# Layer 0's second pass: transposes with both partial sums side by side in place of a folding product

## The reference, cut to what matters

```python
for l in range(n_layers):
    x = jnp.concatenate([h[src], e], axis=1)
    x = x @ W1[l].T + b1[l]
    mu = jnp.mean(x, axis=0)
    var = jnp.var(x, axis=0)
    x = (x - mu) * jax.lax.rsqrt(var + BN_EPS) * gamma[l] + beta[l]
    x = jax.nn.relu(x)
    m = x @ W2[l].T + b2[l]
    h = jax.ops.segment_sum(m, dst, num_segments=n_nodes)
```

## Time and profile before

| | |
|---|---|
| median of 3 runs | 3245.53 us (3243.82 to 3248.12) |
| the profiled execution, its own time | 3253.43 us |
| its span, first to last instruction | 3252.2 us |
| busy share of the span: TensorE, VectorE, ScalarE, GpSimd | 82%, 60%, 41%, 66% |
| mean granted TensorE clock | 0.90 |
| the second pass of layer 0 | 1690.9 to 1869.2 us of the span |

### The profile page before, as it was taken

The page is one execution under the profiler, slowest core; times in us unless marked ns, Lnnn a source line. Parts: engine busy times, 40 slices in busy tenths (PEclk is TensorE's granted clock), DMA queues, the critical chain, the costliest instruction groups (busy, mean ns, idle before and its releaser), DMA issues.

```text
span 3252.2 us, 62180 instructions
## 1 busy us (share of the span) xinstructions
PE 2658.7 (82%) x14706; PEld 1830.4 (56%) x14706; DVE 1961.7 (60%) x3607; ACT 1331.8 (41%) x3295; POOL 2156.6 (66%) x2211
## 2 busy tenths in 40 slices
PE   6689896676777878888889998787879778877998
PEld 2234444555655567677766665555557556655444
DVE  7999585544444567777779965555546555555111
ACT  4877544433333446666657732222223222223111
POOL 4777776777777677777757747777755777774000
PEclk6799997877667889899989999999989999998999
DMA  4333646655555489999958845555535555554100
GB/s 144 103 107 107 199 130 187 189 168 160 166 164 149 136 288 326 319 326 325 324 160 312 295 150 159 155 157 157 158 113 173 156 156 158 156 157 155 52 1 20
DMA packets 305078, 570.49 MB, mean 175 GB/s; under 512 B 54465, under 2 KB 140406, under 8 KB 303510
## 3 DMA queue, kind: packets, MB, share of 16 engines
q1 hardware_dynamic: 204582, 299.39, 29.4%
q0 software_dynamic: 86528, 219.09, 23.1%
q10 hardware_dynamic: 13824, 50.34, 3.9%
HBM read 465.21 MB, written 103.66 MB: 175 GB/s over the span
## 4 chain that ended last, share of the span: by engine, by line
POOL 40%; PE 28%; issue 16%; DVE 7%; DMA 4%; DVEq 2%; ACT 2%; SPq 0%; POOLq 0%; ACTq 0%
POOL region L534 20%; POOL tN L534 11%; PE psum L959 9%; POOL tA L534 9%; PE psum L611 4%; DVE region L1491 2%; PE psum L1216 2%; PE psum L625 2%; PE psum L1205 2%; PE psum L917 1%; PE psum L772 1%; DVEq L1484 1%; PE psum L932 1%; DMA tN<-tabs,region 1%; PE psum L783 1%
## 5 line engine op out<-in xcount | busy, mean ns | idle before, releaser
L534 POOL DMA_INDIRECT region<-tab,region x624 | 601.3, 964 | 271.3 <-issue 197.3
L1205 PE MATMUL psum<-w_all,region 128*128 128x256 f32 x2496 | 632.4, 399 | 3.1 <-DVE small L1894 2.4
L1205 PEld LDWEIGHTS psum<-w_all,region 128*128 128x128 f32 x2496 | 482.1, 200 | 67.1 <-issue 3.8
L2607 POOL DMA_INDIRECT by_tile<-stage,place x416 | 408.5, 982 | 167.6 <-issue 129.1
L657 ACT COPY win_turned<-psum 128x128 f32<-128x128 f32 x210 | 55.7, 265 | 803.4 <-PE psum L641 803.4
L534 POOL DMA_INDIRECT tN<-tab,region x312 | 299.7, 961 | 95.0 <-issue 94.7
L534 POOL DMA_INDIRECT tA<-tab,region x312 | 296.5, 950 | 95.0 <-issue 94.7
L611 PE MATMUL psum<-region 128*64 128x256 f32 (+1 forms) x1664 | 222.5, 392 | 165.6 <-DVE region L2010 97.4
L1216 PE MATMUL psum<-region 128*128 128x256 f32 x1040 | 281.1, 417 | 78.3 <-DVE region L1871 72.4
L1216 PEld LDWEIGHTS psum<-region 128*128 128x128 f32 x1040 | 206.9, 206 | 132.4 <-issue 101.4
L2005 DVE TENSOR_TENSOR psum<-region,psum 128x1024 f32<-128x1024 f32 x104 | 127.9, 1229 | 212.2 <-DMA region<-tab,region 201.4
(11 more groups left out here) (423 smaller groups left out, 5251.4 us busy)
## 6 DMA issues: line engine op xcount, KB each, us to landing
region<-e_t SPq DMA_DIRECT2D x416, 256.0 KB
region<-by_tile SPq DMA_DIRECT2D x131, 264.0 KB
stage<-e_rows SPq DMA_DIRECT2D x208, 132.0 KB
pre_dram<-region ACTq DMA_DIRECT2D x48, 512.0 KB, 6.0
pre_dram<-tN ACTq DMA_DIRECT2D x48, 512.0 KB, 5.8
region<-pre_dram SPq DMA_DIRECT2D x48, 512.0 KB
tN<-pre_dram SPq DMA_DIRECT2D x48, 512.0 KB, 4.8
tA<-dst_row SPq DMA_DIRECT2D x78, 256.0 KB
```

Source lines behind the costliest of these rows:

```text
L534: pool.indirect_dma_start(ring[j][:, c, at:at + width], None, table[:, :], bass.IndirectOffsetOnAxis(ap=idx[:, c:c + 1], axis=0)).then_inc ...
L1205: mm = pe.matmul(banks[:, 2 * (j % 2) + c // 2, (c % 2) * 256:(c % 2) * 256 + 256], e_ring[:, j % E_SLOTS, c * D:(c + 1) * D], W(f"ee{l}") ...
L2607: pool.indirect_dma_start(by_tile[:, :], bass.IndirectOffsetOnAxis(ap=place[:, 2 * q + c:2 * q + c + 1], axis=0), stage[:, k, c, :], None) ...
```

## The change

In layer 0's second pass, `pe_turn_window` is replaced by `pe_turn_halves` and `dve_window` by `dve_halves`. TensorE transposes each half of `win_ring` as it is, 128 x 128, so both partial sums stand side by side in PSUM, and `window_ps` becomes 256 columns wide. VectorE adds the first partial sums of both halves to `acc`, waits for its own addition (a semaphore counted by `wide_done`, which this stage did not use), and adds the second ones. The semaphore that frees the PSUM bank for TensorE (`sc_add`) comes from the second addition.

```diff
         def window_ps(slot):
-            return banks[:, 2 * slot + 1, 0:2 * WIN]
+            return banks[:, 2 * slot + 1, 0:4 * WIN]
...
-            T.add(msg=NG, oh_off=NG, oh_sq=NG)
+            T.add(msg=NG, oh_off=NG, oh_sq=NG, wide_done=NG + LAG)
...
+        def pe_turn_halves(pe, T, b, slot):
+            pe.wait_ge(S["win_out"], T["win_out"] + b + 1)
+            pe.wait_ge(S["sc_add"], T["sc_add"] + b + LAG - 2)
+            pe.nop(nofuse=True)
+            for h in range(2):
+                mm = pe.transpose(window_ps(slot)[:, h * D:(h + 1) * D], win_ring[:, slot, h * D:(h + 1) * D], ident[:, :])
+            mm.then_inc(S["win_t"], 1)
+
+        def dve_halves(dve, T, a, w0, slot):
+            dve.wait_ge(S["win_t"], T["win_t"] + a - (LAG - 2))
+            dve.wait_ge(S["sc_add"], T["sc_add"] + a)
+            to = acc[:, 0:2, bass.ds(w0, WIN)]
+            turned = window_ps(slot).rearrange("p (h k n) -> p h k n", h=2, k=2)
+            dve.tensor_tensor(to, to, turned[:, :, 0, :], ALU.add).then_inc(S["wide_done"], 1)
+            dve.wait_ge(S["wide_done"], T["wide_done"] + a + 1)
+            dve.nop(nofuse=True)
+            dve.tensor_tensor(to, to, turned[:, :, 1, :], ALU.add).then_inc(S["sc_add"], 1)
...
                         pe_window(pe, T, g, j, 2)
-                        pe_turn_window(pe, T, g, (j + 1) % 2, 2)
-                pe_turn_window(pe, T, NG, (NG + 1) % 2, 2)
+                        pe_turn_halves(pe, T, g, (j + 1) % 2)
+                pe_turn_halves(pe, T, NG, (NG + 1) % 2)
...
                         dve_wide(dve, T, wide, g, sums2)
-                        dve_window(dve, T, g, w0, (j + LAG) % 2, 2)
+                        dve_halves(dve, T, g, w0, (j + LAG) % 2)
                 scale_out(l, vrow_mm)
                 for a in range(NG, NG + LAG):
-                    dve_window(dve, T, a, dve_window_start(dve, a - LAG), (a + LAG) % 2, 2)
+                    dve_halves(dve, T, a, dve_window_start(dve, a - LAG), (a + LAG) % 2)
```

## The result

The changed kernel takes 3265.54 us (median of 6 runs, 3262.75 to 3266.79), against 3244.27 us for the kernel before on the same chip (6 runs, 3239.38 to 3248.12). The ratio of the runs is 1.0058, 95% interval 1.0045 to 1.0072 (the two medians alone give 1.0066): 21 us or 0.6% slower. The forecast was 3276.5 in a range of 3259 to 3295. The way and the mechanism were right, the size was too large by half.

A forecast was written before the change was run, and what follows sets the result against it. The prediction took TensorE (1.60 us a group) as the bound, then VectorE at 1.96. Pass +31.0, clearings +0.2, the rest nothing: +31 on the median 3245.5 gives 3276.5 us, range 3259 to 3295.

The forecast's parts named there:

- The bound moves to VectorE: Full-clock stretch of the pass: VectorE at 1.96 us a group binds, above TensorE's 1.33; chance 0.80.
- The +31 us: Whole kernel: pass end moves from 1869.2 to 1900.2 us, +31.0, clearings +0.2, rest of the program nothing.
- The pair at 0.51: VectorE, first to second addition: 0.29 for the addition plus 0.22 for the wait, 0.51 us start to start.
- Maximum to addition at 1.22: VectorE's group: 1.22 us from the start of a maximum to the start of the addition behind it.
- TensorE's group: Window products and turn: 1.60 us a group falls to 1.33 at full clock, 2.95 to 2.53 at half clock.
- The 0.31 for the hand-over: TensorE's turn at full clock: of its 0.59 us, some 0.31 is hand-over between the two kinds of weights.
- The start and the end: Half clock until about 1711.1 us, VectorE then at maximum 9.05 instead of 8; 3.8 us after the last maximum.
- GpSimd: Its 0.61 us instruction fits into the 0.7 us gap between maxima, so the maximum takes 1.22; otherwise add 9 us.
- The DMA share: Transfers in the full-clock stretch: share falls from 0.92 to about 0.75; they need 1.47 us a group.
- The wait is free: Rival on VectorE's two additions: pair costs 0.20, group 1.65 us, 3248 us in all, no difference; chance 0.06.
- Faster through cover: Rival: second addition adds less than 0.14 us to VectorE's group, transfers and VectorE's 1.46 bind, 3230 us; chance 0.03.
- The clock falls: Rival: TensorE's granted clock falls to half throughout, TensorE binds at 2.53 us a group, +88, 3334 us; chance 0.06.

## Why the prediction was right, and where its size was off

**The bound moves to VectorE: right, and shown.** The run with one addition and the run with the folding product and two additions take the change apart: the first isn't slower than before, the second has the changed kernel's 1.779 a group exactly. The +31 us were 21, and two terms of the group were mis-sized.

**The pair at 0.51: too dear, the largest miss.** It measures 0.39. I had taken the 0.22 between the folding product's end and a waiting addition as the price of the wait. That path has a message from another engine and the address of the addition in it. Behind VectorE's own addition the address is already there (no FUSED_REGOPS row for line 652). The lower bound, 0.36 from the earlier trace rows, was the nearer row: the same engine, its own semaphore. The extra `nop` costs 0.02 to 0.03 over it, not 0.15. 0.12 too much in each of some 94 groups is 11 us.

**Maximum to addition at 1.22: too long by up to 0.08.** I read it at the loop edge, the one place where VectorE wasn't waiting for TensorE, but where its queue had only just come round the loop. In the steady stretch it is 1.14, and 1.17 where one more register operation stands in the queue. Together with the pair, the group is 1.78 instead of 1.96, some 17 us of the sum.

**TensorE's group: nearly right, and off the path.** At the half clock it is 1694.97 - 1692.45 = 2.52 us for the 2.53 of the sum. At the full clock it is 1.38 for 1.33: the turn falls from 0.59 to 0.37 us, by 0.22 and not 0.27. The sum took two starts of 0.11 to 0.13 "plus a little"; it is just the two starts. The 0.31 for the hand-over doesn't follow from its rows either: 0.59 less three steps of 0.13 leaves 0.20. Since VectorE binds, neither reached the forecast.

**The start and the end.** The clock came back after 6.4 us of the pass instead of 20, and VectorE was two groups further by 1711 us than the sum had it: 3.4 us less. The end took 5.4 us behind the last maximum instead of 3.8, since TensorE's last turn waits for the pair before it (1.21 us, "DVE acc L652"):

```profile
1878.91 0.41 PE L641 MATMUL psum<-ident,region 128*128 128x128 f32 x2 [1.21 <-DVE acc L652]
```

31 - 17 - 3.4 + 1.6 = 12, which is what the two profiles differ by.

**From the profile to the median.** I put the difference, worked out against a profile 8 us above the median, on the median as it was. With the clock's short stretch in both, the difference of the passes is 18.7. The two errors partly cancelled: the terms were too large by 19 us, and the profile's own excess over the median hid some 9 of them, 6.5 by the long stretch in the pass. So the range was met with some luck. Between the two profiles that the sum speaks of, the pass grew by 12.2 us and not by 31, and 12.2 on the median would have been 3257.7, just below the range's 3259.

**GpSimd: right.** Its subtraction fell from 1.18 to 1.51 us to 0.72 to 1.36, and the maximum stayed at 1.22 in the steady stretch. The reason is the turns seen above: in the changed kernel, GpSimd's turn falls into the pair and is over before the next maximum. The DMA share did not fall to 0.75 but to 0.87: it does not go with the rate (0.92 at 327 GB/s, 1.00 at 380).

**The rivals.** *The wait is free* falls by the run without it, and its price was wrong too: with a free wait the group would have been 1.55, a gain of 0.2%. *Faster through cover* had its floor wrong: at 1.55 the turns of VectorE and GpSimd bind, above the 1.46 and 1.47 that I gave for VectorE alone (measured: 1.38) and for the transfers. The most that this change could have brought in the steady stretch is 0.05 x 104 = 5 us. *The clock falls* did not come in the pass: 1.00 in the whole steady stretch, with TensorE at 1.38 of work in 1.78. "TensorE: Matmul & The Clock Gate", "Part 4: PE-mode transpose", of the Trainium skill says that the full clock doesn't engage for transposes. Between products, as here, they made no difference to the clock that these traces show. Right behind the pass the granted clock did fall, to 0.50 from 1881.4 to 1884.8 us, behind two idle stretches of TensorE of 1.21 and 2.21 us. The transposes aren't needed for that, for the run with the folding product and two additions shows it too. The kernel before has only 0.91 us of idle time there and keeps 1.00. The run with four additions keeps it too, with 0.76 and 2.17 us idle, so what decides it stays open; in the totals outside the pass it doesn't show.

## What to carry to other kernels

Before work is moved off the bounding engine, write down the floor of every other engine in that loop; here three stood between 1.38 and 1.60 us a group (VectorE alone, VectorE with GpSimd, TensorE). VectorE had 0.2 us of room, and 0.05 with GpSimd's turns, for a pair of dependent additions that costs 0.59 where the single one cost 0.20. Two engines that take turns need their times added, not compared. Price a wait by the nearest row of the same kind (own engine or another's, address known or not), and take an engine's own cycle from where nothing holds it, not from a loop's edge. Where TensorE bounds, look at several profiles of the same kernel for the place of its half-clock stretch before a difference of a few us is read from two of them.

## What the runs showed of the hardware

VectorE and GpSimd, each with two inputs in SBUF, take turns. GpSimd's subtraction (0.61 us alone) that starts inside a maximum ends 0.47 us behind the maximum's end, and takes up to 1.70 us for it (changed kernel, 1699.95). A maximum (1.22) that starts inside a subtraction takes up to 1.64. With one addition, or two without a wait, the two engines settle at 1.553 us a group. Only the amount of GpSimd's work was varied here, not the place of its inputs, so what they take turns for is not shown.

A wait of VectorE for its own addition of 128x128 (0.28 us long) makes 0.39 from start to start, where 0.20 is usual. An addition of 128x64 with one input in PSUM starts 0.13 us behind another, one of 128x128 0.20, so small VectorE instructions can fill a wait at little cost.
